# Attention's last query tile: its probabilities in another buffer, and three instructions in another place of their queues

## The reference, cut to what matters

```python
x = x + L0_conv(_gn(x), ...)      # stem, three pooling levels, 1x1 convs, four
                                  # depthwise taps per channel tile, gate, 1x1 conv
x = x + L1_conv(_gn(x), w1, w2)

def L1_conv(x, w1, w2):           # f: (b, 1024, 256)
    q = einsum('bnc,dc->bnd', f, w1)
    attn = einsum('bnd,bmd->bnm', q, f) * scale
    attn = softmax(attn, axis=-1)
    v = einsum('bnc,dc->bnd', f, w2)
    return einsum('bnm,bmd->bnd', attn, v)
```

## Time and profile before

| | us |
|---|---|
| median of three runs | 1384.13 |
| lowest and highest | 1377.48, 1387.42 |
| profiled execution, its own time | 1376.88 |
| span of the trace | 1375.1 |
| PE busy (share of the span) | 1206.2 (88%) |
| DVE busy | 1152.7 (84%) |
| ACT busy | 726.0 (53%) |
| mean granted clock of PE | 0.96 |

### The profile page before, as it was taken

The page is one execution under the profiler, slowest core; times in us unless marked ns, Lnnn a source line. Parts: engine busy times, 40 slices in busy tenths (PEclk is TensorE's granted clock), DMA queues, the critical chain, the costliest instruction groups (busy, mean ns, idle before and its releaser), DMA issues.

```text
span 1375.1 us, 17821 instructions
## 1 busy us (share of the span) xinstructions
PE 1206.2 (88%) x6730; PEld 1026.1 (75%) x6730; DVE 1152.7 (84%) x1220; ACT 726.0 (53%) x781; POOL 293.6 (21%) x247
## 2 busy tenths in 40 slices
PE   3559898766899999999899999999998999999697
PEld 1249898655678877877788788878887887797597
DVE  7779887799989889989998999899989977985343
ACT  0246667663375447536753675366546643853342
POOL 1566767401111111111111111111111111000000
PEclk9769999987999999999999999999999999999899
DMA  7403123253665566566456644764475466001000
GB/s 287 168 31 93 77 86 115 97 126 90 142 143 118 151 177 122 113 169 160 107 121 197 141 109 108 208 140 104 116 200 126 108 144 157 0 1 62 0 0 31
DMA packets 72303, 159.91 MB, mean 116 GB/s; under 512 B 33088, under 2 KB 35904, under 8 KB 72256
## 3 DMA queue, kind: packets, MB, share of 16 engines
q0 software_dynamic: 23904, 92.11, 29.9%
q1 hardware_dynamic: 47648, 66.85, 14.7%
q10 hardware_dynamic: 704, 0.30, 0.1%
HBM read 41.46 MB, written 25.17 MB: 48 GB/s over the span
## 4 chain that ended last, share of the span: by engine, by line
PE 36%; DVE 18%; issue 17%; ACT 6%; DMA 3%; DVEq 0%; POOL 0%; ACTq 0%; POOLq 0%
PE slot L1299 12%; PE slot L1246 10%; PE ps_level L1299 10%; DVE between L1574 4%; PE slot L1315 3%; DVE a L1574 2%; DMA boxes<-twos 2%; DVE pt_all L345 1%; ACT a L1478 1%; ACT between L1428 1%; DVE f_all L410 1%; DVE x L1617 1%; ACT f_all L1447 1%; ACT a L1428 1%; DVE tall L323 1%
## 5 line engine op out<-in xcount | busy, mean ns | idle before, releaser
L1299 PE MATMUL ps_level<-v_all,pt_all 128*128 128x256 f32 x1536 | 200.1, 287 | 13.6 <-DVE pt_all L1578 8.2
L1299 PEld LDWEIGHTS ps_level<-v_all,pt_all 128*128 128x128 f32 x1536 | 189.6, 192 | 17.3 <-DVE pt_all L1578 15.8
L1299 PE MATMUL slot<-f_all,q_all 128*128 128x512 f32 x768 | 189.7, 397 | 0.0
L1574 DVE SCALAR_TENSOR_TENSOR a<-between,k_columns,a 128x992 f32<-128x992 f32 (+1 forms) x128 | 157.6, 1232 | 6.9 <-ACT a L1428 4.6
L1299 PEld LDWEIGHTS slot<-f_all,q_all 128*128 128x128 f32 x768 | 140.1, 188 | 27.9
L1578 DVE TENSOR_TENSOR pt_all<-slot,pt_all 128x1024 fp32r<-128x1024 f32 x64 | 78.2, 1221 | 40.8 <-ACT pt_all L1442 40.6
L1451 ACT CAST v_all<-y 128x1024 fp32r<-128x1024 f32 x32 | 33.8, 1055 | 134.6 <-DVE y L1607 134.4
L1456 ACT ACTIVATE mixed<-ps_level,row_inv 128x256 f32<-128x256 f32 x64 | 30.2, 473 | 133.5 <-PE ps_level L1299 133.5
L1428 ACT ACTIVATE a<-between,k_columns 128x1024 f32<-128x1024 f32 x64 | 79.3, 1240 | 33.3 <-DVE between L1574 32.3
L1607 DVE SCALAR_TENSOR_TENSOR y<-slot,k_columns,y 128x1024 f32<-128x1024 f32 x32 | 40.9, 1282 | 57.0 <-PE slot L1246 55.1
L1574 DVE SCALAR_TENSOR_TENSOR between<-y,k_columns,between 128x992 f32<-128x992 f32 x64 | 78.8, 1249 | 7.8 <-ACT between L1428 6.6
(11 more groups left out here) (204 smaller groups left out, 2752.1 us busy)
## 6 DMA issues: line engine op xcount, KB each, us to landing
levels<-x_all SPq DMA_DIRECT2D x32, 512.0 KB, 2.6
boxes<-twos POOLq DMA_DIRECT2D x28, 543.0 KB, 4.8
boxes<-twos POOLq DMA_DIRECT2D x28, 527.0 KB, 4.6
x_all<-in_x SPq DMA_DIRECT2D x8, 1024.0 KB, 12.8
f_all<-levels SPq DMA_DIRECT2D x8, 1024.0 KB, 7.4
x<-in_x SPq DMA_DIRECT2D x8, 1024.0 KB, 5.9
out<-x SPq DMA_DIRECT2D x8, 1024.0 KB, 4.1
twos<-boxes POOLq DMA_DIRECT2D x14, 561.0 KB, 3.0
```

Source lines behind the costliest of these rows:

```text
L1299: last = nc.tensor.matmul(out, lhs, rhs, start=(n == 0), stop=(n == len(parts) - 1))
L1574: nc.vector.scalar_tensor_tensor(o, u, keep["taps"][:, s, c, tap:tap + 1], o, ALU.mult, ALU.add).then_inc(taps.sem, 1)
```

## The change

Four edits, all in phase c. The list `probs` gives tiles 0 to 6 the old buffer and tile 7 the buffer `early`; exponent(7) therefore waits for its maximum alone and no longer for `turned` of tile 6. On ACT, exponent(7) stands first in tile 7, ahead of scale_mixed(5) and turned_hi(6), where it stood behind both. On DVE, maximum(7) stands between the two outer taps of stage 14 instead of behind them (only where there is a convolution); and turned_lo(7) stands right behind turned_lo(6), ahead of the outer taps of stage 15, invert(7), add_attention(5). PE's queue is unchanged but for the buffer that turn(7) reads.

```diff
-        prob = pooled.second
+        probs = [pooled.second] * (TILES - 1) + [chain.early]
...
-                        last = nc.tensor.transpose(slot[:, cols(m)], prob[:, cols(m)], keep["ident"][:, :])
+                        last = nc.tensor.transpose(slot[:, cols(m)], probs[t][:, cols(m)], keep["ident"][:, :])
...
                 def exponent(t):
                     wait(act, maxed, i - 1, t + 1)
-                    if t:
+                    if t == 0:
+                        wait(act, pooled.lo_done, i - 1, 2)
+                    elif t < TILES - 1:
                         wait(act, turned, i - 1, t)
-                    else:
-                        wait(act, pooled.lo_done, i - 1, 2)
-                    nc.scalar.activation(prob[:, :], slots_of["s", t][:, :], ACT.Exp, bias=minus_max[:, t:t + 1],
+                    nc.scalar.activation(probs[t][:, :], slots_of["s", t][:, :], ACT.Exp, bias=minus_max[:, t:t + 1],
...
                     for t in range(TILES):
+                        if t == TILES - 1:
+                            exponent(t)
                         if t > 1:
                             scale_mixed(t - 2)
                         if t:
                             turned_hi(t - 1)
                         if t == 1 and conv:
                             centre_tap(BEFORE + 1)
-                        exponent(t)
+                        if t < TILES - 1:
+                            exponent(t)
...
-                def outer_taps(n):
+                def outer_taps(n, *ks):
...
-                    for k, tap in ((0, 0), (1, 2)):
+                    for k in ks or range(2):
+                        tap = 2 * k
...
-                        if conv and t:
+                        if t == TILES - 1:
+                            turned_lo(t)
+                        if conv and t == TILES - 2:
+                            outer_taps(BEFORE + t, 0)
+                            maximum(t + 1)
+                            outer_taps(BEFORE + t, 1)
+                        elif conv and t:
                             outer_taps(BEFORE + t)
-                        if t + 1 < TILES:
+                        if t + 1 < TILES and not (conv and t == TILES - 2):
                             maximum(t + 1)
...
-                    turned_lo(TILES - 1)
```

## The result

The changed kernel takes 1368.17 us (median of 8 runs, 1365.54 to 1369.42); the kernel before, run as often, 1382.41 us (1377.33 to 1387.45). The ratio is 0.9889, 95% interval 0.9865 to 0.9914: 1.1% faster, where 0.4% was forecast and the range ended at 1370.0.

What follows compares the result with a forecast made beforehand. PE (88% busy) and DVE (84%) were taken to bound the kernel in turns. Eight gains of 0.69 us, 5.5 in all, took 1376.88 to 1371.4 us, ratio 0.9960; scaled to the median, 1378.6 us, range 1370 to 1386.

Steps and rivals of the forecast that it cites:

- the local sum: End of each attention: mix(6) starts 0.69 us earlier, held by turned_lo(6); 8 x 0.69 = 5.5 us gained.
- the second gate: In c1 behind attention: it waits 1.66 us for PE, so the 0.69 us go through.
- the first gate: In c1 behind attention: DVE's own time without a gap, so it doesn't come earlier.
- no DMA wait at the last mixture: Last mixture at 642.06: its box sum lands early enough; of 2.4 us of slack 1.7 stay.
- POOL and SP without effect: SP's load of `pooled` goes out about 2 us earlier; POOL's wait of 12.20 us covers the box-sum transfer.
- The rival that the whole bubble goes: End of attention: mix(6) right behind turn(7), 2.0 us earlier; 15.9 us gained, 1368.1 us; chance 0.05.
- the clock's term: PE's clock in the last attention's mix(6): at most 1.5 us more gained if it stays at 2.4 GHz, 1377.1 us.
- the third rival: End of attention: PE's clock falls as idle time is broken up, +5.0 us, 1389.1 us; chance 0.04.
- the scaling to the median: Whole kernel: the profiled execution's ratio 0.9960 applied to the median of 1384.13 us, giving 1378.6 us.
- without this edit mix(7) keeps 0.1 us: End of attention: without the earlier turned_lo(7), mix(7) would wait until 591.86 us instead of starting at 591.78.

Runs made afterwards that it cites:

- filled by 12: Kernel before with 12 identity transposes ahead of turn(7) in PE's queue, nothing else moved: 1373.53 us, ratio 0.9941.
- filled by 6: Kernel before with 6 identity transposes ahead of turn(7) in PE's queue: 1373.75 us, ratio 0.9916.
- late maximum: Changed kernel with maximum(7) back behind both outer taps of stage 14: 1372.83 us, ratio 0.9928 to the kernel before.
- turned_lo(7) late: Changed kernel with turned_lo(7) back in its old place behind all of tile 7: 1369.48 us, ratio 0.9915 to the kernel before.
- hi products first: Kernel before with mix's 16 products that need only turned_hi(t) ahead of the 8 that read turned_lo(t): 1369.06 us, ratio 0.9908.

## Why the prediction was wrong, and where it was right

**Right: the local sum.** The prediction named turned_lo(6) as the next thing late and put mix(6) 0.69 us earlier; measured are 0.71. It had the whole of it passed on to mix(7) (measured 0.69) and the second gate (0.72), the first gate unmoved (14.80 us), no DMA wait at the last mixture, POOL and SP without effect, and so it was. For the idle time ahead of mix(6) it had 1.2 to 1.3 us in 8 times, "about 10 us"; it is 8 x 1.27 = 10.2. The rival that the whole bubble goes is refuted as a mechanism, although the time measured is the one it gave (1368.1), which is chance: the idle time of PE fell by 0.71 us per attention, not by 2.

**Wrong: the clock's term.** The sum took 0 for it, and 1.5 us as its upper bound, from one long mix(6) in the last attention against seven short ones. The step that failed is the sentence that in the second attention the same stall left the clock at 1.00 and mix(6) took 3.11 or 3.12 us in all seven. That was true of that execution, and it was taken for the kernel. In five profiled executions of kernels with the stall of 1.99 us, the ends were long 1, 5, 1, 4 and 4 times of 8: 15 of 40. In eight of kernels whose longest stall is at most 1.34 us, 0 of 64. Three kernels that bring no instruction ahead of mix(6) earlier, or in seven of eight attentions by 0.14 us only (filled by 12, filled by 6, late maximum), gained 0.0059, 0.0084 and 0.0072, or 8 to 12 us. The change's 0.0111 less its local 0.0040 is 0.0071, in line with them.

Long ends alone would have to be five to seven of eight in a median execution of before to make these 8 to 12 us, and five was the most seen. The falls ahead of the q products fill a part of the gap. The profiled execution of before at 1384.07 us, close to its median, and the one of the changed kernel at 1368.96 lie 15.1 us apart in their spans. The waits make 5.6 of it, five long ends against none 5 x 1.57 = 7.9, and five falls at the q products against two 3 x 0.7 = 2.1: 15.6. That the change makes the falls at the q products rarer is not shown: PE's wait there is as long in every kernel, and they were 3, 5, 3, 4 and 4 of 6 in the executions with the stall of 1.99 us, 2 to 4 of 6 in the nine others. So of about 14 us gained, 5.6 are waits and most of the rest is the clock behind the ended stall.

**Wrong: the sign of the third rival.** It had the clock fall after the change, because idle time is broken up. Breaking it up did no harm: 0.76 and 0.85 us with work between left the clock up in all attentions, 1.99 in one piece didn't in 15 of 40. Whether the piece or the total counts stays open, for where the pieces were short the total was shorter too (1.61 against 1.99 us). The Trainium skill's page TensorE: Matmul & The Clock Gate, in its section on psum-queue depth-cycling, speaks of frequent short idle times; here short ones did no harm, and the one long piece did. The rule of the Trainium skill's page Perfetto Trace Analysis, Optimization Strategy, that a repeated gap can mean too few buffers, didn't hold by itself: the second buffer alone changed nothing that could be measured (0.9982, 0.9959 to 1.0006).

**Wrong: the scaling to the median.** The profiled execution was 7 us faster than the median, and the prediction carried this over as a factor, as if it were noise common to both kernels. Most of it was a cost that the change removes. The 7 us needed a cause before they were scaled: 1384.13 - 1376.88 = 7.25, four to five falls at the end of attention, or four and two at the q products, as in the execution of 1384.07 us.

**Wrong in size: turned_lo(7).** The prediction says that without this edit mix(7) keeps 0.1 us. It compares 591.86 with 591.78, which means that 0.1 is lost and about 0.6 kept. The run with turned_lo(7) late measured 0.12 lost; its own expectation repeated the slip.

**What stays open.** Which attentions are hit varies from execution to execution of the same kernel, and nothing here fixes it. The spread between runs is not told by the long ends: it is 11 us in the kernel filled by 12, whose two profiled executions have none, and 3 us in the kernel before with hi products first, whose profiled execution has four. Of the kernel filled by 6, the execution of 1379.84 us is partly explained (5.5 us ahead of 478 us). Whether the change alters the falls ahead of the q products, 0.7 us each, would take more profiled executions than there are.

## What to carry to other kernels

When the profiled execution and the median of the runs lie apart by more than the change is to bring, profile again until an execution near the median is seen, and find what differs, before anything is summed. A stall that repeats on PE had two prices here: its length, and the clock behind it, which was paid in some attentions and executions only. Ask of a change how long the longest piece is that it leaves: every fall between 400 and 1280 us followed a wait of 1.76 us or more. And when a product waits for the last of several operands, let the products of the earlier ones go first: here a new order of 24 instructions brought more than the change did.

## What the runs showed of the hardware

- At the end of attention, the granted clock fell to 0.50 (the 1.2 GHz level) behind a stall of 1.99 us of PE in 15 of 40 cases, and not always in the same attentions; behind 1.76 to 1.82 us in 1 of 6; behind 0.66 to 1.34 us in 0 of 64. Such a fall cost 1.57 us from turn(7) to mix(7).
- Behind the wait of 2.18 to 2.33 us ahead of the q products it fell in 42 of 84 cases, at about 0.7 us each. Behind the wait of mix for turned_lo early in six attentions, 1.33 to 1.40 us in 70 cases, it never fell; in the two cases in which that wait was 2.10 and 2.45 us, it did.
- 96 transposes that compute nothing, put into the stalls of 1.99 us, made the kernel 0.6% faster (0.9916 to 0.9966).
- In the changed kernel's profiled execution scale_mixed(5) found ACT free: exponent(7) with its accumulator read ended at 584.12 + 0.19 = 584.31 and it started at 584.39. No engine showed the tighter order as a delay.
